# A graph kernel's edge counting: item offsets packed into one word per group, unpacked inside the address expression

## What is computed

```python
res = jax.ops.segment_sum(w[:, :, None] * v, rows, num_segments=nvar)   # layer 0, attention over edges
h_e = jax.ops.segment_sum(h[src], dst, num_segments=h.shape[0])         # layer 2
return jax.ops.segment_sum(wn[:, None] * h[row], col, num_segments=n)   # layer 3, three times
```

## Time and profile before

| what | value |
|---|---|
| median of 3 runs | 1393.35 us (1390.63 to 1393.75) |
| profiled execution, its own time | 1392.31 us |
| its span on the core | 1390.6 us |
| TensorE matmul busy | 1101.8 us, 79% |
| VectorE busy | 986.4 us, 71% |
| ScalarE busy | 706.9 us, 51% |
| GpSimd busy | 572.0 us, 41% |

### The profile page before, as it was taken

The page is one execution under the profiler, slowest core; times in us unless marked ns, Lnnn a source line. Parts: engine busy times, 40 slices in busy tenths (PEclk is TensorE's granted clock), DMA queues, the critical chain, the costliest instruction groups (busy, mean ns, idle before and its releaser), DMA issues.

```text
span 1390.6 us, 23439 instructions
## 1 busy us (share of the span) xinstructions
PE 1101.8 (79%) x8345; PEld 640.9 (46%) x8345; DVE 986.4 (71%) x1647; ACT 706.9 (51%) x908; POOL 572.0 (41%) x332
## 2 busy tenths in 40 slices
PE   3887877777599478788878787884687899999993
PEld 2545544555355122122222222221587897778783
DVE  8678888876534389999989989886956554432366
ACT  7555565556221499899989898983100000000121
POOL 8433525231000629899989998983000000000000
PEclk9879799789589689999999999997689899999996
DMA  0000000000133111111111112111111000010201
GB/s 11 30 29 5 8 5 9 4 16 1 47 77 90 49 32 44 44 33 56 34 45 41 50 47 56 42 55 35 44 43 59 27 26 1 1 31 7 63 27 35
DMA packets 61246, 47.28 MB, mean 34 GB/s; under 512 B 31276, under 2 KB 59564, under 8 KB 61008
## 3 DMA queue, kind: packets, MB, share of 16 engines
q1 hardware_dynamic: 59440, 44.04, 11.0%
q0 software_dynamic: 1696, 1.74, 0.5%
HBM read 31.96 MB, written 13.79 MB: 33 GB/s over the span
## 4 chain that ended last, share of the span: by engine, by line
PE 52%; DVE 21%; ACT 13%; issue 9%; POOL 2%; another core or an unknown queue 1%; DMA 0%; SPq 0%; DVEq 0%; ACTq 0%; POOLq 0%
PE PS L1346 17%; DVE Eb L1152 12%; PE PS L553 10%; PE PS L557 7%; ACT Eb L1117 6%; ACT Eb L1119 5%; PE PS L1702 3%; PE PS L1066 2%; PE PS L886 2%; PE PS L1055 2%; PE PS L870 1%; POOL Eb L993 1%; PE PS L1337 1%; ACT Eb L1121 1%
## 5 line engine op out<-in xcount | busy, mean ns | idle before, releaser
L993 POOL TENSOR_SCALAR Eb<-Eb 128x1024 f32<-128x1024 f32 (+4 forms) x164 | 403.5, 2475 | 65.4 <-ACT Eb L1121 65.2
L1152 DVE SCALAR_TENSOR_TENSOR Eb<-Eb,PS 128x1024 f32<-128x1024 f32 (+4 forms) x350 | 365.1, 1083 | 46.6 <-ACT Eb L1119 31.4
L1346 PE MATMUL PS<-hs,CT 128*128 128x192 f16 (+3 forms) x2500 | 269.5, 271 | 6.0 <-DVE B L1547 2.7
L1121 ACT ACTIVATE Eb<-PS,small 128x1024 f32<-128x1024 f32 (+5 forms) x257 | 246.7, 994 | 29.8 <-PE PS L1066 16.4
L593 ACT ACTIVATE CT<-PS 128x500 f32 x313 | 183.7, 587 | 144.6 <-PE PS L557 135.9
L1346 PEld LDWEIGHTS PS<-hs,CT 128*128 128x128 f16 (+1 forms) x2500 | 233.0, 101 | 39.4 <-DVE B L1547 3.2
L553 PE MATMUL PS<-mov,oneS 128*128 128x100 f16 x1565 | 185.7, 231 | 77.2 <-issue 73.9
L553 PEld LDWEIGHTS PS<-mov,oneS 128*128 128x128 f16 x1565 | 146.8, 107 | 159.4 <-issue 116.7
L1066 PE MATMUL PS<-Qb,Kb 96*128 96x512 f16 (+3 forms) x700 | 198.1, 365 | 25.3 <-issue 11.1
L1076 PE MATMUL PS<-Eb,V 128*25 128x512 f32 (+3 forms) x1400 | 170.8, 560 | 2.9 <-DVE Eb L1152 2.9
L435 DVE TENSOR_TENSOR oneS<-iotaX,KL 128x2560 f16<-128x2560 int16 x80 | 120.3, 1504 | 72.3 <-PE PS L557 70.4
(11 more groups left out here) (259 smaller groups left out, 1025.4 us busy)
## 6 DMA issues: line engine op xcount, KB each, us to landing
Kb<-kd SPq DMA_DIRECT2D x168, 96.0 KB
qd<-QH SPq DMA_DIRECT2D x24, 96.0 KB, 1.9
kd<-QH SPq DMA_DIRECT2D x24, 96.0 KB, 2.2
XG<-x_d SPq DMA_DIRECT2D x12, 192.0 KB, 2.4
x_d<-XG SPq DMA_DIRECT2D x12, 192.0 KB, 1.8
hs<-t_d SPq DMA_DIRECT2D x12, 192.0 KB, 2.5
Qb<-qd SPq DMA_DIRECT2D x4, 384.0 KB
CT<-x_d SPq DMA_DIRECT2D x1, 1200.0 KB, 7.5
```

What stands on the lines that cost most here:

```text
L993: g.tensor_scalar(e, e, ELO, None, ALU.max).then_inc(S("floored"), 1)
L1121: a.activation(e, ps, ACT.Exp, scale=K.unsc[0:r, :]).then_inc(S("score_read"), 1)
L1152: v.scalar_tensor_tensor(out=e, in0=e, scalar=EHI, in1=cn, op0=ALU.min, op1=ALU.mult).then_inc(S("weighed"), 1)
L1346: m = p.matmul(bank(t % FIRST)[0:r, 0:w], K.CT[:, a, 128 * t:128 * t + r], hs[:, a, :, :].rearrange("p k d -> p (k d)"), start=(a == 0), s ...
```

## The change

The four offsets of a group become fields of one word: the first destination in bits 0 to 11, the offset of item k divided by 4 in the three bits from 9 + 3k. `table(h)` builds the word in floating point by four multiply-and-adds on every fifth column of the row, and casts it. TensorE and ScalarE both load 4 words a set. The first destination is `word % 4096`, an offset `(word // 2 ** (9 + 3 * k)) % 8 * 4`, both written into the address expression.

```diff
-    K.wI = [sb(st, "wI%d" % h, [b - a, BLOCK], I32) for h, (a, b) in enumerate(PARTS)]
+    K.wI = [sb(st, "wI%d" % h, [b - a, BLOCK // GI], I32) for h, (a, b) in enumerate(PARTS)]
+    K.wF = sb(st, "wF", [8, BLOCK // GI], F32)
...
     def table(h):
 
+        n = PARTS[h][1] - PARTS[h][0]
         v.wait_ge(S("windows"), h + 1)
-        v.tensor_copy(K.wI[h][:, :], K.bank(4)[0:PARTS[h][1] - PARTS[h][0], 128:128 + BLOCK]).then_inc(S("reg_set"), 1)
+        ps = K.bank(4)[0:n, 128:128 + BLOCK].rearrange("p (g k) -> p k g", k=GI)
+        v.tensor_copy(K.wF[0:n, :], ps[:, 0, :]).then_inc(step, own.up())
+        for k in range(1, GI):
+            v.wait_ge(step, own.n)
+            v.scalar_tensor_tensor(out=K.wF[0:n, :], in0=ps[:, k, :], scalar=2.0 ** (9 + 3 * k) / W, in1=K.wF[0:n, :],
+                                   op0=ALU.mult, op1=ALU.add).then_inc(step, own.up())
+        v.wait_ge(step, own.n)
+        v.tensor_copy(K.wI[h][:, :], K.wF[0:n, :]).then_inc(S("reg_set"), 1)
...
-def load_windows(K, e, ety, s, every):
+def load_words(K, e, ety, s):
...
-    j, o = s // 6, SET * (s % 6)
+    j, o = s // 6, 4 * (s % 6)
...
-        K.wI[h][r:r + 1, o:o + SET:every], engines=[ety], min_val=0, max_val=W * (NW - 3),
+        K.wI[h][r:r + 1, o:o + 4], engines=[ety], min_val=0, max_val=2 ** 24 - 1,
...
+def first_of(word):
+    return (word % 4096).with_bounds(min_val=0, max_val=W * (NW - 3))
+
+
+def further(word, k):
+    return (((word // 2 ** (9 + 3 * k)) % 8) * W).with_bounds(min_val=0, max_val=(GI - 1) * W)
...
-            words = load_windows(K, t, mybir.EngineType.PE, s, 1)
+            words = load_words(K, t, mybir.EngineType.PE, s)
...
-            to = ps[:, :, 0:W] if k == 0 else ps[:, :, bass.ds(vals[k], W)]
+            to = ps[:, :, 0:W] if k == 0 else ps[:, :, bass.ds(further(word, k), W)]
...
-        t.matmul(ps, K.identb[:, :], K.CT[:, :, bass.ds(vals[0], GI * W)], start=False, stop=True, skip_group_check=True
+        t.matmul(ps, K.identb[:, :], K.CT[:, :, bass.ds(first_of(word), GI * W)], start=False, stop=True, skip_group_check=True
...
-            words = load_windows(K, a, mybir.EngineType.Activation, s, GI)
+            words = load_words(K, a, mybir.EngineType.Activation, s)
...
-        a.activation(K.CT[:, :, bass.ds(words[g % 4][0], GI * W)],
+        a.activation(K.CT[:, :, bass.ds(first_of(words[g % 4]), GI * W)],
```

More of the change, by code:

```diff
@@ L484, in load_windows @@
     e.wait_ge(K.S("reg_set"), h + 1)
-    _, vals = K.nc.values_load_multi_w_load_instructions(
-        K.wI[h][r:r + 1, o:o + SET:every], engines=[ety], min_val=0, max_val=W * (NW - 3),
[L487 to L490, removed]
+    _, words = K.nc.values_load_multi_w_load_instructions(
+        K.wI[h][r:r + 1, o:o + 4], engines=[ety], min_val=0, max_val=2 ** 24 - 1,
+        skip_runtime_bounds_check_because="the words are made by words() from the staircase")
+    return words
+def first_of(word):
+    return (word % 4096).with_bounds(min_val=0, max_val=W * (NW - 3))
+def further(word, k):
+    return (((word // 2 ** (9 + 3 * k)) % 8) * W).with_bounds(min_val=0, max_val=(GI - 1) * W)
 def build_tensor(t, K):
@@ L545, in build_tensor @@
         if g % 4 == 0:
-            words = vals = to = None
-            words = load_windows(K, t, mybir.EngineType.PE, s, 1)
+            words = load_words(K, t, mybir.EngineType.PE, s)
             t.wait_ge(S("one_hot"), s + 1)
-        vals = words[g % 4]
+        word = words[g % 4]
         ps = bank(g % 4)[:, 0:25 * GI * W].rearrange("p (a c) -> p a c", a=25)
         for k in range(GI):
-            to = ps[:, :, 0:W] if k == 0 else ps[:, :, bass.ds(vals[k], W)]
+            to = ps[:, :, 0:W] if k == 0 else ps[:, :, bass.ds(further(word, k), W)]
             t.matmul(to, K.oneS[:, s % DEEP, o + k, :], K.mov[:, s % DEEP, o + k, :].rearrange("p (a w) -> p a w", a=25),
```

## The result

The changed kernel takes 1427.59 us (1425.07 to 1434.67, 4 runs) against 1391.99 us (1390.59 to 1393.75, 4 runs) of the kernel before on the same chip: a ratio of 1.0263, 95% interval 1.0224 to 1.0303. It is slower by 35.6 us.

The account below looks back on a forecast made before the run. TensorE's own instruction stream was taken to bound the counting stage. Full-clock sets +26.3 us, low-clock sets -1.4 and the table +0.5 gave +25.4 us, a median of 1418.8 us; its own range was 1393 to 1470, the whole reaching down to 1378.

Parts of the forecast that it names:

- its own case: Address chains of the counting stage: each quotient or remainder costs 15 to 43 ns, taken as 25; chance 0.50.
- (a): TensorE's register load at each set's start falls from 20 registers to 4: -465 ns a set, all exposed.
- (b): Each of 16 offset chains a set gains quotient, remainder and product: 59 ns a chain, 944 ns a set.
- (c): Each of 4 identity-matmul chains a set gains a remainder: 100 ns on TensorE; ScalarE's chain gains one as well.
- The wait of 0.1 us a set: TensorE's waiting on ScalarE within a set, taken back by a slower sequencer: -100 ns in each full-clock set.
- The low clock: 25 counting sets at low clock: later groups need 882 ns of sequencer against the array's 833; -57 ns a set, -1.4 us.
- (d): Table building on VectorE: one cast becomes six small instructions, +1.0 us in each of three places, mostly covered; +0.5 us.
- (e): VectorE's one-hots, 1.49 + 1.19 us a set, stay below the set's period, so only the sequencer is late.
- 1: Cheap members: quotient and remainder in the address chains cost an add's 9 ns; 1380 us, faster; chance 0.26.
- 2: Dear members: quotient and remainder in the address chains cost 50 ns each; 1491 us; chance of more than 43 ns 0.11.
- 3: The six-member chain in banks 1 to 3 doesn't fit one instruction; 12 chains a set pay 98 ns more; 1513 us; chance 0.08.
- 4: The sequencer has cover in the counting stage, so time moves from load to chains and nothing changes; 1393 us; chance 0.05.

Follow-up runs that it names:

- the small quotients: Changed kernel with each item's offset as word // (2**21 + k) times 4, a three-bit quotient without remainder; 1364.18 us, 0.9887 of the kernel before.

## Why the prediction was right, and where its terms were not

The forecast was +25.4 us and 1418.8; measured were +35.6 and 1427.59, in the range. The mechanism was the forecast's: the sequencer paces, and chains cost more than loads save. Its break-even lay near 15 ns a member and its own case was 15 to 43 ns; taken as half of what a quotient and a remainder add together (133 to 143 ns, less 46 and 9), a member measured 39 to 44, at the upper edge of that case. That the sum came as near as it did is luck in part: two terms were far off, by 45 us and by 35 us, with opposite signs.

- **(a) The load**: taken -465 ns a set from ScalarE's load of four; measured -1028, 82.4 us in all instead of 37.2. The mistake is the row: ScalarE's four lay five columns apart, and stride, not the start of a load, made 895 ns of it. (1360 - 332) / 16 is 64 ns a register for neighbours, not the 29 of the forecast. The fact stood in the kernel's own slice, `o:o + SET:every`.
- **(b), (c) The members**: taken at 25 ns, a quotient and a remainder measured 35 to 38 each among their like and, in the changed kernel's mixed order, 39 to 44; the chains grew by 118.9 us in place of 80 x 1.044 = 83.5. The 29 ns that drew me to 25 was itself the wrong price of (a), and that a quotient is done in many steps was my reason, which no run shows; they show its price. One guess was right: the third member is 9 ns. One thing was overlooked: the top field needs no remainder, as the word's bound of 2^24 - 1 already gives it three bits, and the built program holds 939 remainders for offsets, three a group, and none for item 4.
- **The wait of 0.1 us a set** that a slower sequencer takes back: forecast for the 55 sets at full clock, 5.5 us in all. The wait before the identity's chains fell by 6.3 us (9.2 to 2.9), but only 1.5 of the 9.2 lie at full clock, so the size is near and the place is wrong.
- **The low clock**: forecast -1.4 us for 25 sets, as a group at 882 ns was to be near the array's 833. In the kernel before, low-clock groups are 0.83 us apart at the median and those at full clock 0.65, so there the low clock does cost time. The changed kernel's groups are 1.03 us apart at either level: the sequencer's time is above the array's at both, the array hides nothing, and its lower granted clock costs nothing. Had I known (a) alone, I would have forecast a gain; (b) alone, a loss of some 60 us.
- **(d) The table**: +0.5 us foreseen; 0.3 us at the start and 0.9 us in set 1, by the traces. The length of the six steps was right (1.0 us); that the last of them would stand behind GpSimd was not seen.
- **(e)** Held. VectorE's one-hots end after the load of their set once in the kernel before (2.0 us, set 56) and three times in the changed one (1.6 us in set 56, 0.8 in set 1, 0.1 in set 78).
- **Nothing changed behind the stage**: 4.1 us more were measured there, within the spread of this stretch on other chips.
- **The rivals.** 1 fails by its price, and its condition, made real, gives the gain it foretold in kind. 2 (50 ns, from 43 ns up) was nearer to the truth than my 25 in its price. 3 is out: six members are one instruction, 1252 in all. 4 is out as a rule: with 20 registers loaded again, 78 of 82 us showed; it holds for a set like the third, behind 42 extra matmuls. The Trainium skill, page "Advanced Engine Details and Errata", section "Engine Queue Depths", gives the number of instructions that TensorE's queue may hold, 64, and does not say that the sequencer gets ahead. In the stage it gets ahead only where the array has more work than the sequencer; an ordinary group takes 1.03 us of the sequencer and 0.83 of the array even at the low clock, so there is nothing to get ahead of.

## What to carry to other kernels

Where small matmuls take computed addresses, look whether the register work between them is serial time of TensorE's sequencer. Here it is, at these prices: 64 ns to load one more neighbouring number, 37 ns for a quotient or a remainder, some 6 to 17 more for a chain of either behind one of another make, 9 for an add, product or minimum, and 79 for each further address at all. Packing pays only if unpacking a number costs less than the 64 ns of loading it. Quotient, remainder and product (some 87 to 98 ns) cost more; a quotient and a product (44) cost less, and that run was faster than the kernel before (0.9887). What can be added in a table beforehand should be; scaling there was not tried. Before taking a duration from a nearby row, compare its access pattern as well as its count.

## What the runs showed that was not expected

- A register load by stride: four numbers five columns apart take 995 ns on TensorE and 890 on ScalarE, four neighbours 332 and 308.
- A quotient's price hardly depends on its bits or its divisor (35 to 38 ns), and a remainder among its like costs the same (37 ns). The same chain costs more when the chain before it is of another make: item 4's of the changed kernel 103 ns, the same operations among their like 90; the identity's 88 and 74. Why was not tried.
- A cast of 24 numbers from SBUF to SBUF on VectorE was held for 5.65 us by a GpSimd memset. The Trainium skill, page "SBUF — State Buffer", section "SBUF: two separate sides", says that VectorE in its two-port modes and GpSimd take a shared pair of ports exclusively, for a whole instruction. The trace agrees: 28.98 for the end of the cast, 28.95 for the memset's. A cast that reads PSUM took 0.26 us while the same memset ran; that the held cast ran in such a mode, no trace shows.
- The wait behind that memset is not new. In the kernel before, the first of the four TENSOR_SCALAR of `passes` behind the second table's cast takes 3.95 us (25.20 to 29.15), while the other three take 0.40 to 0.53. It stood behind the one-hots of set 0 there; the change put a cast that waits in front of them.

```profile
25.20 5.08 DVE L398 TENSOR_SCALAR past<-iotaS,le 128x720 f16<-128x720 int16 x4
```

- The granted clock of the stage was 0.85 before, 0.77 changed, 0.63 with both the long load and the long chains, and 0.97 in the stage of the small quotients. It doesn't follow the pace of the groups alone: those of the kernel before come fastest of these four and have 0.85. In the kernel before the low level cost time, in the changed kernel it didn't.
